# A four-layer kernel on one core: foldings and own keys moved in the opening, and the pieces of the last three steps re-ordered on every engine

## The reference, cut to what matters

```python
# layer 0: attention of side rows (queries) over x (keys), own key added, 16 heads of 16
q = (side + b_self) @ Wq + bq
k = concat([x + b_prev, side + b_self]) @ Wk + bk ; v = concat([x, side]) @ Wv + bv
w = softmax(concat([mask(q @ k_prev.T) / 4, (q * k_self).sum(-1) / 4]))
x = x + (w[:, :-1] @ v_prev + w[:, -1:] * v_self) @ Wo + bo
# layer 1: adapter of 64, with a layernorm
h = relu(x @ W1[lang] + b1[lang])
x = x + layernorm(x + h @ W2[lang] + b2[lang]) * gamma[lang] + beta[lang]
# layer 2: a linear layer by subject
x = x + x @ weight[subj].T + bias[subj]
# layer 3: pooling with one score a token, under a prefix, postfix or cloze mask
s = tanh(x @ W1 + b1) @ v
p = softmax(where(mask[kind], s, -1e30))
x = x + (p @ x) / count
```

## Time and profile before

| | before |
|---|---|
| time, median of 3 runs | 950.7 us (949.37 to 950.89) |
| the profiled execution's own time | 947.73 us |
| its span, first to last instruction | 945.7 us |
| PE busy | 914.1 us (97%) |
| DVE, ACT, POOL busy | 694.5, 642.8, 602.1 us |
| mean granted clock of TensorE | 0.991 |

### The profile page before, as it was taken

How to read it: one execution, slowest core, us unless ns; L and a number is a source line. 1 busy time by engine, 2 the same in 40 slices (tenths; PEclk the granted TensorE clock), 3 DMA queues, 4 the chain that set the end, 5 groups by cost and what they waited for, 6 DMA issues and landing times.

```text
span 945.7 us, 28023 instructions
## 1 busy us (share of the span) xinstructions
PE 914.1 (97%) x8631; PEld 767.8 (81%) x8631; DVE 694.5 (73%) x1612; ACT 642.8 (68%) x1381; POOL 602.1 (64%) x767
## 2 busy tenths in 40 slices
PE   8899999999999999999999999999999999999867
PEld 7787788888888888888888888888888888887566
DVE  8666777787777778777777877777777777777453
ACT  4456677777667777776777777677777767766632
POOL 4344667777666777666677766667676666665551
PEclk9999999999999999999999999999999999999989
DMA  7344434444443444444344444433444544332221
GB/s 261 132 139 136 141 109 128 144 143 152 147 132 107 132 141 144 147 152 130 107 128 147 138 147 157 125 112 125 150 133 147 158 130 125 127 117 87 82 68 41
DMA packets 113209, 124.55 MB, mean 132 GB/s; under 512 B 23541, under 2 KB 95110, under 8 KB 113158
## 3 DMA queue, kind: packets, MB, share of 16 engines
q1 hardware_dynamic: 111384, 121.22, 40.7%
q10 hardware_dynamic: 1774, 2.68, 0.9%
HBM read 63.99 MB, written 8.96 MB: 77 GB/s over the span
## 4 chain that ended last, share of the span: by engine, by line
PE 82%; issue 8%; DVE 5%; ACT 3%; POOL 1%; DVEq 1%; DMA 0%; ACTq 0%; POOLq 0%
PE M L471 26%; PE ST L574 10%; PE PV L471 9%; PE PV L553 7%; PE M L479 7%; PE SN L578 5%; PE M L782 5%; PE M L605 3%; DVE mx L1309 3%; PE M L659 3%; ACT x1T L1002 2%; PE M L741 2%; PE M L731 1%; PE M L626 1%; PE SN L813 1%
## 5 line engine op out<-in xcount | busy, mean ns | idle before, releaser
L1309 DVE TENSOR_REDUCE mx<-SN 128x2 f32<-128x512 f32 x504 | 324.4, 686 | 73.1 <-PE SN L578 73.1
L1026 ACT ACTIVATE pt<-ST 128x512 f32<-128x512 f32 x512 | 277.9, 599 | 80.6 <-PE ST L574 79.0
L574 PE MATMUL ST<-qst,kst 64*128 64x256 f32 x1024 | 187.3, 304 | 12.1 <-DVE mx L1309 6.6
L574 PEld LDWEIGHTS ST<-qst,kst 64*128 64x128 f32 x1024 | 135.8, 185 | 67.8 <-issue 28.1
L578 PE MATMUL SN<-kst,qst 63*128 63x256 f32 x1008 | 183.8, 304 | 0.7 <-issue 0.7
L578 PEld LDWEIGHTS SN<-kst,qst 63*128 63x128 f32 x1008 | 132.7, 185 | 1.3 <-issue 0.9
L553 PE MATMUL PV<-pt,vaug 128*32 128x256 f32 x2048 | 124.2, 383 | 0.1
L866 POOL TENSOR_TENSOR ss<-xsin,ss 128x512 fp32r<-128x512 f32 x32 | 40.9, 1278 | 120.7 <-ACT ss L1002 113.7
L553 PEld LDWEIGHTS PV<-pt,vaug 128*32 128x32 f32 x2048 | 60.1, 110 | 43.2 <-issue 5.5
L471 PE MATMUL M<-lwp,x2T 128*128 128x320 f32 x378 | 69.0, 319 | 0.9 <-issue 0.9
L866 POOL TENSOR_TENSOR x2T<-x2f,x2T 128x512 fp32r<-128x512 f32 x31 | 39.9, 1288 | 44.0 <-ACT x2T L1002 44.0
(11 more groups left out here) (185 smaller groups left out, 2086.6 us busy)
## 6 DMA issues: line engine op xcount, KB each, us to landing
qst<-qp SPq DMA_DIRECT2D x186, 128.0 KB
kst<-kp SPq DMA_DIRECT2D x186, 128.0 KB
xsin<-in_xsT SPq DMA_DIRECT2D x31, 512.0 KB, 3.4
adw<-in_wad SPq DMA_DIRECT2D x32, 322.5 KB, 4.0
pm<-in_pmask SPq DMA_DIRECT2D x32, 257.0 KB, 2.7
xr<-in_x SPq DMA_DIRECT2D x32, 256.0 KB, 4.2
lwf<-in_lwT SPq DMA_DIRECT2D x32, 256.0 KB, 3.2
out<-ob SPq DMA_DIRECT2D x31, 256.0 KB, 2.2
```

The source lines that it names most:

```text
L574: keys = nc.tensor.matmul(ST[e][:, half * S:half * S + S], kst[par][lo_:lo_ + MROW + 1, pair, half * P:half * P + P], qst[par][lo_:lo_ + M ...
L1026: nc.scalar.activation(pt[:, g, :, j, :], ST[s % 2][:].rearrange("p (h q) -> p h q", h=2), ACT.Exp, scale=SCALE).then_inc(sem("exp_done"), 1)
L1309: nc.vector.tensor_reduce(out=mx[odd][:, :, 8 * (s // 8) + PH * (1 - s % 2) + s // 2 % PH], in_=(ST if isinstance(t, int) and t == -1 and ...
```

## The change

In the opening: the first folding (`h` of step 0) is issued on PE at the end of step -1; in step 0 `own_keys` comes between `scores(0)` and `scores(1)`, and the `ad` folding follows `scores(1)`. In the tail: the order of the pieces is another one on each engine; there are 59 filler matmuls in place of 79; `x3` of item 30 also gets a place in `pt`, and so does the mask of item 31, which then waits for `pv_done` in place of `masked` and `r3`; POOL's `w` waits for `ad_pe` behind its first instruction.

```diff
@@ tiles
-        x3_last = pt[:, 0, 0, :, :].rearrange("p j q -> p (j q)")[:, 0:2 * NX].rearrange("p (i n) -> p i n", i=2)
+        x3_late = [pt[:, 0, k, :, :].rearrange("p j q -> p (j q)")[:, 0:2 * NX].rearrange("p (i n) -> p i n", i=2)
+                   for k in range(2)]
-            return x3_last if isinstance(b, int) and b == B - 1 else x3
+            return x3_late[b % 2] if isinstance(b, int) and b >= B - 2 else x3
+        pm_late = pt[:, 1, 0, :, :].rearrange("p j q -> p (j q)")[:, 0:2 * (S + 1)].rearrange("p (i n) -> p i n", i=2)
+        def pm_of(b):
+            return pm_late if isinstance(b, int) and b == B - 1 else pm
@@ SP, piece pm
-                    sp.wait_ge(sem("masked"), done(t - 4))
-                    sp.wait_ge(sem("r3"), done(t - 4))
-                    sp.dma_start(pm[:], pm3[ki]).then_inc(sem("ld_pm"), 16)
+                    if isinstance(t, int) and t == B + 2:
+                        sp.wait_ge(sem("pv_done"), done(B - 1, 2))
+                    else:
+                        sp.wait_ge(sem("masked"), done(t - 4))
+                        sp.wait_ge(sem("r3"), done(t - 4))
+                    sp.dma_start(pm_of(t - 3)[:], pm3[ki]).then_inc(sem("ld_pm" if not isinstance(t, int) or t < B + 2 else "ld_pm_late"), 16)
@@ SP, tail
+            step(B, 0, "lwf")
             step(B, 0, "xr")
-            step(B, 0, "lwf")
             step(B, 0, "pm")
             step(B, 0, "lbr")
+            step(B + 1, 1, "lwf")
             step(B + 1, 1, "pm")
-            step(B + 1, 1, "lwf")
             step(B, 0, "out")
@@ PE, opening
                     scores(7)
+                    pe.wait_ge(sem("kf"), done(t + 2))
+                    fold_gate(FOLD[0], 0)
                     return
...
                 scores(0)
                 if go("E", "pv1"):
                     weighted(1, t - 1, odd)
+                first = isinstance(t, int) and t == 0
+                if first:
+                    own_keys()
                 scores(1)
-                if on["B"]:
+                if first:
+                    fold_next("ad")
+                elif on["B"]:
                     own_keys()
-                if folding(t):
+                if folding(t) and not first:
                     fold_next("h")
...
-                if folding(t):
+                if folding(t) and not first:
                     fold_next("ad")
@@ PE, tail (the order after)
             step(B, 0, "num")
             keep_busy(10)
             step(B, 0, "aT")
             step(B, 0, "h")
             step(B, 0, "srep")
             step(B, 0, "wo")
             step(B, 0, "ad")
             step(B, 0, "x1T")
             step(B, 0, "pT")
             keep_busy(4)
             step(B + 1, 1, "h")
             keep_busy(5)
             step(B, 0, "x2T")
             keep_busy(4)
             step(B + 1, 1, "ad")
             step(B, 0, "pool")
             step(B, 0, "lin0", "lin1")
             step(B + 1, 1, "x2T")
             keep_busy(8)
             step(B + 1, 1, "srep")
             keep_busy(6)
             step(B + 1, 1, "lin0", "lin1")
             keep_busy(8)
             step(B + 1, 1, "pT")
             step(B + 2, 0, "srep")
             step(B + 1, 1, "pool")
             keep_busy(8)
             step(B + 2, 0, "pT")
             keep_busy(6)
             step(B + 2, 0, "pool")
@@ POOL, piece w
+                    late = isinstance(t, int) and t == B
+                    if not late:
+                        pool.wait_ge(sem("ad_pe"), done(t - 2))
-                    pool.wait_ge(sem("ad_pe"), done(t - 2))
                     hi(w1p[0][:], twice).then_inc(sem("whi"), 1)
+                    if late:
+                        pool.wait_ge(sem("ad_pe"), done(t - 2))
                     hi(w2p[0][:], w2raw[odd]).then_inc(sem("whi"), 1)
@@ DVE, third
-                    if isinstance(b, int) and b == B - 1:
-                        dve.wait_ge(sem("pv_done"), done(b, 2))
+                    if isinstance(b, int) and b >= B - 2:
+                        dve.wait_ge(sem("pv_done"), done(B - 1, 2))
```

More of the change, by code:

```diff
@@ L819, in _ @@
             step(B, 0, "num")
+            keep_busy(10)
+            step(B, 0, "aT")
             step(B, 0, "h")
             step(B, 0, "srep")
-            keep_busy(4)
-            step(B, 0, "aT")
+            step(B, 0, "wo")
             step(B, 0, "ad")
+            step(B, 0, "x1T")
             step(B, 0, "pT")
             keep_busy(4)
-            step(B, 0, "wo")
+            step(B + 1, 1, "h")
             keep_busy(5)
-            step(B, 0, "x1T")
+            step(B, 0, "x2T")
+            keep_busy(4)
+            step(B + 1, 1, "ad")
             step(B, 0, "pool")
-            step(B + 1, 1, "h")
-            step(B, 0, "x2T")
+            step(B, 0, "lin0", "lin1")
+            step(B + 1, 1, "x2T")
             keep_busy(8)
-            step(B + 1, 1, "ad")
-            step(B, 0, "lin0", "lin1")
             step(B + 1, 1, "srep")
-            keep_busy(14)
-            step(B + 1, 1, "x2T")
+            keep_busy(6)
+            step(B + 1, 1, "lin0", "lin1")
+            keep_busy(8)
             step(B + 1, 1, "pT")
-            keep_busy(14)
-            step(B + 1, 1, "lin0", "lin1")
+            step(B + 2, 0, "srep")
             step(B + 1, 1, "pool")
-            keep_busy(6)
-            step(B + 2, 0, "srep")
-            keep_busy(18)
+            keep_busy(8)
             step(B + 2, 0, "pT")
@@ L982, in _ @@
             step(B - 1, 1)
+            step(B, 0, "eyed")
             step(B, 0, "xb")
-            step(B, 0, "eyed")
             step(B, 0, "tvv")
+            step(B, 0, "lwlo")
+            pool.wait_ge(sem("lwlo"), done(B - 2))
             step(B, 0, "hlo")
@@ L989, in _ @@
             step(B, 0, "x1b2")
-            step(B, 0, "lwlo")
+            step(B + 1, 1, "eyed")
             step(B, 0, "x2Tlo")
-            step(B + 1, 1, "eyed")
+            step(B + 1, 1, "rstd")
             step(B + 1, 1, "tvv")
-            step(B + 1, 1, "rstd")
             step(B + 1, 1, "lwlo")
@@ L1429, in step @@
                     dve.wait_ge(sem("srep_pe"), done(t - 3))
-                    dve.wait_ge(sem("ld_pm"), done(t - 3, 16))
+                    if isinstance(t, int) and t == B + 2:
+                        dve.wait_ge(sem("ld_pm_late"), 16)
+                    else:
+                        dve.wait_ge(sem("ld_pm"), done(t - 3, 16))
                     dve.wait_ge(sem("pe3"), done(t - 4, 2))
                     nc.vector.tensor_tensor(msc[:], place("srep", t)[:, 0:S].unsqueeze(1).to_broadcast([P, 2, S]),
-                                            pm[:, :, 0:S], ALU.add).then_inc(sem("masked"), 1)
+                                            pm_of(t - 3)[:, :, 0:S], ALU.add).then_inc(sem("masked"), 1)
                     dve.wait_ge(sem("masked"), done(t - 3))
@@ L1535, in _ @@
             step(B, 0, "sc")
+            step(B, 0, "aTlo")
             step(B, 0, "masked")
-            step(B, 0, "aTlo")
+            step(B, 0, "x1")
             step(B, 0, "y")
@@ L1540, in _ @@
             step(B, 0, "aggr")
-            step(B, 0, "x1")
+            step(B, 0, "x1Tlo")
             step(B, 0, "r3")
-            step(B, 0, "x1Tlo")
-            step(B, 0, "x2f")
-            step(B, 0, "outs")
             dve.wait_ge(sem("hf"), done(B - 1))
@@ L1549, in _ @@
                                     ALU.subtract).then_inc(sem("hlo"), 1)
+            step(B, 0, "x2f")
             step(B + 1, 1, "y")
@@ L1552, in _ @@
             step(B + 1, 1, "aggr")
+            step(B, 0, "outs")
             step(B, 0, "x3a")
             step(B + 1, 1, "x3b")
+            step(B + 1, 1, "x2f")
             step(B + 1, 1, "sc")
-            step(B + 1, 1, "masked")
-            step(B + 1, 1, "x2f")
             dve.wait_ge(sem("x2Thi"), done(B - 1))
@@ L1560, in _ @@
             nc.vector.tensor_tensor(x2T[1][:], x2f[:], x2T[0][:].bitcast(F32), ALU.subtract).then_inc(sem("x2Tlo"), 1)
-            step(B + 1, 1, "r3")
+            step(B + 1, 1, "masked")
             step(B + 1, 1, "x3a")
             step(B + 2, 0, "x3b")
-            step(B + 1, 1, "outs")
             step(B + 2, 0, "sc")
             step(B + 2, 0, "masked")
+            step(B + 1, 1, "r3")
+            step(B + 1, 1, "outs")
             step(B + 2, 0, "r3")
```

20 lines of the change are left out of this document (11 added, 9 removed).

## The result

| | before | after |
|---|---|---|
| time, median | 950.8 us (4 runs, 949.37 to 951.3) | 934.54 us (4 runs, 933.92 to 934.71) |
| ratio to before | | 0.9835 (95% interval 0.982 to 0.9851) |
| the profiled execution: time, span | 947.73, 945.7 us | 934.71, 933.1 us |
| mean granted clock of it | 0.991 | 0.998 |

What follows compares the result with a forecast made beforehand. PE's own work bounds the middle, so only waits and clock falls at the two ends were counted: opening 3.5 plus tail 9.9 make 13.4 us, 950.7 to 937.3. Own range 935.5 to 940; for 8 in 10, up to 941.5.

Steps and rivals of the forecast that it cites:

- 2.69 + 0.91 - 0.1: Opening: scores(2) earlier by 2.69, second folding out of the way 0.91, wait at scores(3) 0.1; sum 3.5 us.
- DVE's products and join: Opening, step 0: products (0.88) and join (0.3) between DVE's maxima make PE wait about 0.1 us at scores(3).
- The stacked keys: Opening: keys of batch 1, issued by 33.2 on SP, wanted at 37.7 instead of 41.2; a possible late load.
- The rival that the loop swallows it: Stack load or maxima row at its old time in step 0 or 1 swallows the opening's gain: 940.8, chance 0.12.
- The clock: Both ends: full clock expected, no PE idle above 1 us before 930 in the tail; rival of falls 941.7, chance 0.17.
- Link 1: Tail, loads to aTlo: xr issued 2.1 us later, landing 4.5 after issue, costs 1.0 us; aTlo at 904.2.
- Links 2 to 4: Tail, batch 31: x1 at 906.7 (gain 3.85), relus end at 912.8 (4.9), yn starts at 917.65 (8.5).
- Link 5: Tail, yn to lin of batch 31: 4.3 us instead of 4.99, lin at 921.95, gain 9.2.
- Link 6: Tail, lin to last pooling: 2.04 unchanged, then 6.75 instead of 7.48, r3 of 30 costing 0.4; pooling 930.75, gain 9.9 us.
- The own places: Tail: separate places for x3 of 30 and mask of 31 cost nothing, avoiding waits for the batch before's tanh and pooling.
- 950.7 - 13.4: Whole kernel: gain of 13.4 us taken off the median of the runs shown, 950.7, giving 937.3.
- The slower rival: PE at half clock through the whole new tail: span 946 to 949 against 945.7; chance 0.02.

Runs made afterwards that it cites:

- run 3: Kernel before, nothing moved, with 8 filler matmuls in the opening's first gap and 10 in the second: 948.13 us, ratio 0.996.
- run 6: Kernel before, order kept, with more fillers in its tail's idle stretches (45 added): 948.23 us, ratio 0.9966.
- run 4: Kernel after without any of the tail's 59 filler matmuls: 939.01 us, ratio 0.9861.
- run 2: Kernel after with its opening put back as before, so the tail's change alone: 939.94 us, ratio 0.9892.
- run 7: Kernel after with r3 of item 30 moved on DVE to right behind x3b of item 31: 934.76 us.
- run 11: Kernel of run 7 with the mask of item 31 in its old tile, loaded behind masked and r3 of item 30: 936.43 us.
- run 10: Kernel after with x3 of item 30 in its old place, with its old waits: 935.35 us.
- run 8: Kernel after with xr loaded ahead of lwf on SP and xb ahead of eyed on POOL: 935.59 us.

## Why the prediction was right, and where it was off

- **The opening** (2.69 + 0.91 - 0.1) came as worked out: 2.68 at `scores(2)`, 3.58 at step 1. DVE's products and join cost PE nothing at `scores(3)`. The stacked keys were in time. The rival that the loop swallows it fell: it comes out at the start of the tail less 0.28.
- **The clock.** That it would hold in both ends was right, 1.00 all through. Its part is 1.5 us of the opening (run 3) and 3.3 of the tail (run 6), the rest is order. Run 4 shows that the new order needs the fillers for it.
- **Link 1** was wrong in its terms and came out right in sum, by luck. `xr` landed 3.15 us after its issue (894.59 to 897.74), not 4.5 and below the bounds of 3.7 to 6, and so `tvv` was out at 899.89 and not 900.9. Against that `att` on DVE, which the forecast left at its old length, took 1.56 us, since `xb` was running on POOL when it started (undisturbed 0.69, in runs 2 and 7), and `aTlo` waited for ACT's `aThi`. Runs 2 and 7, where `att` started first, show the link without it: the landing again took 3.2 to 3.3 us, `aTlo` went directly behind `sc`, by the path forecast, and came 7.70 us behind the last `pv1`; forecast was 8.41, the kernel after has 8.21. So the landing was 0.7 us too long in the sum, and the stretch took back 0.5 of it.
- **Links 2 to 4** hold to 0.2 us. **Link 5** is 0.5 short, and 0.35 of it is one term: `x2Tlo` on DVE (918.23) took 1.04 us and not 0.69, next to `lwlo` on POOL (917.17 to 918.72). **Link 6** holds, `r3` included, as run 7 shows.
- **The own places "cost nothing"**, true, but I did not say what they bring: for the mask 1.4 to 1.7 us (run 11), for `x3` of 30 nothing (run 10).
- **From the span to the median.** The step that was mis-sized: the measured 934.54 lies below the lower end of the forecast's own range, 935.5. I took the sum of one execution over to the median of the runs (950.7 - 13.4). The profiled execution had a clock that only two of 48 others of the kernel reached; the spans of most are 2 to 6 us longer, at a lower clock, and the kernel after loses almost nothing to it in any. 12.6 by the spans and 16.3 by the medians are both right. The rule that I cited (the Trainium skill, TensorE: Matmul & The Clock Gate, Part 1: the point of the change varies from run to run) bears on the old kernel just as well, and the trace agrees: 945.7 us at 0.991, 952.6 at 0.984. I used it as a risk of the new kernel and left out that the old one already paid.
- **The slower rival** (half clock through the tail) needed the clock to stay low; it was 1.00 throughout. Even with no fillers (run 4) the time stayed 12 us under before's.

Open: in which stretch the executions without a profile lost their clock. Only their mean is known. The profiled ones say that the old opening (7.04 us to `scores(2)` in one, 7.99 in another), step 30 (runs 3 and 4) and step 31 have a share; how large is not settled. Nor is it known why the load came later in run 4 that made its lull longer. That the mean of run 2 goes down to 0.991 with a tail that holds its clock in the profile was not followed up.

## What to carry to other kernels

Where lulls drop TensorE's clock, a profile is one draw: compare its mean clock with those of the timed runs before its spans are carried over to the median. A wait at the ends of a pipelined kernel is worth twice when real work fills it, once for the work and once for the clock behind it, and fillers buy only the second. Where a VectorE instruction with two SBUF inputs and one of GpSimd come due at about the same time, some hundredths of a microsecond decided here which one was held up: see which way it fell before two profiled executions are compared. In a hand-written order, ask of each small op (here `r3`) whether it can go into an idle moment ahead of what waits for it.

## What the runs showed of the hardware

- `att` and `x2Tlo`, VectorE instructions with two SBUF inputs, take 0.69 us with GpSimd out of the way. Where they started while one of GpSimd was running, they ended 0.54 to 0.56 us behind its end, in all 22 such cases behind 890 us in these traces: `att` in 1.56 us (1.01 of it beside `xb`), in 0.89 in run 8 (0.33 beside it), in 0.77 in the kernel before (0.21 beside it), `x2Tlo` in 1.04 (0.49 beside `lwlo`). Each lost its overlap less 0.14 us. Where `att` started first it took 0.69 and `xb` was the one held up: 1.46 us in run 2 and 1.79 in run 7, against 1.26 to 1.29. `tvv`, which came due while `att` ran, took 0.90 against 0.46. The Trainium skill (SBUF — State Buffer, section "SBUF: two separate sides") has it that whichever of the two starts first keeps the shared ports for the whole instruction and the other is blocked; the traces agree in both directions, up to those 0.14 us.
- The same 12 matmuls behind the same lulls took 2.52 us in one execution and 1.69 in another (run 3 and before, a clock of 0.64 in the 3 us from 859 and of 1.00 in those from 860), and the mean clock of one unchanged kernel ranged over 0.984 to 0.991, its span over 945.7 to 952.6.
